# A decoder layer on one core: two buffers for the mixer's masked products, and level 0 of the next group issued before the finished group is weighed

## The reference, cut to what matters

```python
def step(S, inp):
    q_t, k_t, v_t, w_t = inp
    kv = k_t[..., :, None] * v_t[..., None, :]
    o_t = jnp.einsum('bhk,bhkv->bhv', q_t, S + u[None, :, :, None] * kv)
    S = jnp.exp(w_t)[..., None] * S + kv
    return (S, o_t)
```

## Time and profile before

| what | value |
|---|---|
| median of the runs | 1441.59 us (1439.81 to 1442.03) |
| the profiled execution's own time | 1454.23 us |
| span of that execution | 1452.4 us |
| PE busy | 1316.8 us, 91% of the span |
| DVE, POOL, ACT busy | 934.3, 746.1, 622.5 us |
| mean granted clock of PE | 0.967 |

### The profile page before, as it was taken

One profiled execution on the slowest core, in us unless ns is written; L12 is line 12 of the kernel. 1 busy time (PEld: TensorE's weight loads), 2 busy tenths in 40 slices (PEclk: granted clock), 3 DMA queues, 4 the chain that ended last, 5 costly groups with the idle time before them and its releaser, 6 DMA issues.

```text
span 1452.4 us, 30935 instructions
## 1 busy us (share of the span) xinstructions
PE 1316.8 (91%) x9852; PEld 889.5 (61%) x9853; DVE 934.3 (64%) x1964; ACT 622.5 (43%) x1519; POOL 746.1 (51%) x1080
## 2 busy tenths in 40 slices
PE   5789998999749999999999999999988999999996
PEld 3456655666535666666666666666655566666664
DVE  2587787777614888888888888888884322222221
ACT  2455544554313555555555555555543221211221
POOL 5234443243144678777787777877754322222222
PEclk9999999999757999999999999999999999999998
DMA  4996000000026554545544545545532322222221
GB/s 143 281 318 176 1 1 1 0 1 1 1 64 88 106 118 120 122 123 124 124 101 120 122 124 126 117 121 125 117 85 59 56 45 44 47 45 46 44 44 22
DMA packets 152749, 127.80 MB, mean 88 GB/s; under 512 B 41630, under 2 KB 145510, under 8 KB 152614
## 3 DMA queue, kind: packets, MB, share of 16 engines
q1 hardware_dynamic: 140310, 112.02, 31.3%
q0 software_dynamic: 12304, 14.10, 6.3%
HBM read 35.90 MB, written 44.83 MB: 56 GB/s over the span
## 4 chain that ended last, share of the span: by engine, by line
PE 56%; DVE 8%; issue 3%; ACT 2%; DMA 1%; SPq 0%; another core or an unknown queue 0%; POOL 0%; DVEq 0%; ACTq 0%; POOLq 0%
PE bank_st L1948 10%; PE bank_v L1966 7%; PE bank_s L1780 6%; PE bank_v L1768 6%; PE bank_o L1810 4%; PE bank_st L1790 4%; DVE neg_raw L1469 4%; PE bank_m L1743 4%; PE bank_s L1948 3%; PE bank_m L1832 2%; PE bank_st L1799 2%; DVE bank_st L1480 2%; PE bank_o L1957 2%; PE bank_v L1758 1%; PE bank_m L1820 1%
## 5 line engine op out<-in xcount | busy, mean ns | idle before, releaser
L1469 DVE TENSOR_REDUCE neg_raw<-bank_s 100x2 f32<-100x722 f32 x256 | 229.4, 896 | 32.1 <-PE bank_s L1780 30.2
L1316 ACT ACTIVATE prob<-bank_st 120x400 f32<-120x400 f32 (+1 forms) x384 | 166.2, 513 | 159.4 <-PE bank_st L1799 159.4
L1256 POOL DMA_INDIRECT out<-result,target x57 | 88.4, 1550 | 234.4 <-DVE result L1686 186.0
L1480 DVE TENSOR_SCALAR bank_st<-bank_st 121x1200 f32<-121x1200 f32 x128 | 180.3, 1408 | 1.2 <-PE bank_st L1790 0.8
L1681 DVE TENSOR_TENSOR hidden<-silu,bank_st 128x512 f32<-128x512 f32 x57 | 39.2, 688 | 192.7 <-PE bank_st L1948 192.7
L1948 PE MATMUL bank_st<-expert_w,rows_t 128*128 x344 | 159.3, 599 | 0.7 <-issue 0.5
L409 ACT ACTIVATE q_heads<-q 32x192 f32<-32x192 f32 (+3 forms) x224 | 82.7, 369 | 140.8 <-DVE q L521 136.4
L1780 PE MATMUL bank_s<-k_st,q_st 96*128 96x361 bf16 x512 | 124.1, 324 | 15.5 <-DVE neg_raw L1469 10.1
L1155 POOL TENSOR_TENSOR neg_diag<-xident_b,neg_max 100x400 bf16<-100x400 bf16 x128 | 109.4, 855 | 47.6 <-DVE neg_max L1474 47.0
L741 PE MATMUL bank_l<-q_heads,k 128*100 128x192 f32 (+4 forms) x512 | 114.9, 366 | 18.7 <-ACT q_heads L409 7.3
L293 POOL TENSOR_TENSOR mixed<-part,xn_t 128x400 f32<-128x400 f32 x80 | 84.4, 1080 | 82.0 <-DVE part L462 81.9
(11 more groups left out here) (231 smaller groups left out, 2545.8 us busy)
## 6 DMA issues: line engine op xcount, KB each, us to landing
k_st<-k_part SPq DMA_DIRECT2D x384, 90.2 KB
slot_rows<-empty SPq DMA_DIRECT2D x9, 2967.0 KB, 26.3
q_st<-q_part SPq DMA_DIRECT2D x192, 50.0 KB
kv<-in_ctx_t SPq DMA_DIRECT2D x32, 270.8 KB
expert_w<-in_w SPq DMA_DIRECT2D x16, 512.0 KB
rows<-slot_rows SPq DMA_DIRECT2D x57, 129.0 KB
residual<-in_w SPq DMA_DIRECT2D x16, 256.0 KB
residual<-in_x SPq DMA_DIRECT2D x8, 400.0 KB
```

Source lines behind the costliest of these rows:

```text
L1316: act.activation(prob[0:KEYS[c], t % 2, c], bank_st[0:KEYS[c], c, 0:4 * T], ACT.Exp).then_inc(exp_done, 1)
L1469: dve.tensor_reduce(neg_raw[:, h:h + 2], bank_s[0:T, :, 0:S], AX.X, ALU.max, negate=True).then_inc(max_done, 1)
L1480: dve.tensor_scalar(tile, tile, CLAMP, -CLAMP, ALU.min, ALU.max).then_inc(clipped, 1)
```

## The change

`attn` gets a second buffer, and a group uses the one of its parity `p`: in the diagonal copies, in the copies of the later levels and in `weigh`. The second buffer is cleared by GpSimd once, after its work for group 1's normalization, and VectorE waits for that before group 1. The diagonal copies of group g no longer wait for the weighing of g - 1 but for that of g - 2. On PE, `weigh` moves from the head of the body to behind level 0 of batches 0 and 1. On VectorE the diagonal copies of batches 0 and 1 move ahead of the statistics of the first bank. Nothing is added or taken away on PE or ScalarE. The diff, without the lines that only hand on `p`:

```diff
-        attn = sb("attn", [T, G, RH, T])
+        attn = sb("attn", [T, 2, G, RH, T])
...
-            pool.memset(attn[:], 0.0).then_inc(consts, 1)
+            pool.memset(attn[:, 0], 0.0).then_inc(consts, 1)
...
             norm(1)
+            pool.memset(attn[:, 1], 0.0).then_inc(consts, 1)
...
-            def collect(g, lv):
+            def collect(g, p, lv, batches=range(G)):
 
                 if lv == 0:
-                    for j in range(G):
+                    for j in batches:
                         dve.wait_ge(level_summed, g * LEVELS * G + j + 1)
-                        after(dve, o_summed, 2 * g)
+                        after(dve, o_summed, 2 * (g - 1))
                         dve.sem_inc(waited, 1)
-                        dve.copy_predicated(attn[:, j], diagonal[:].unsqueeze(1).to_broadcast([T, RH, T]),
+                        dve.copy_predicated(attn[:, p, j], diagonal[:].unsqueeze(1).to_broadcast([T, RH, T]),
...
+                    if isinstance(g, int) and g == 1 and s == 0:
+                        dve.wait_ge(consts, CONSTS + 1)
                     if s == 0 and not first:
+                        collect(g, p, 0, (0, 1))
                         head_stats(g - 1, 0)
-                    collect(g, s)
-                    if s == 0 and not first:
+                        collect(g, p, 0, (2, 3))
                         head_stats(g - 1, 1)
                         head_moments(g - 1)
+                    else:
+                        collect(g, p, s)
...
             def body(g, p, more):
                 first = isinstance(g, int) and g == 0
-                if not first:
-                    weigh(g - 1, 1 - p)
                 for s in range(LEVELS):
                     if s == 0 and not first:
                         level(g, p, 0, (0, 1))
+                        weigh(g - 1, 1 - p)
                         front(g, 7)
                         level(g, p, 0, (2, 3))
```

More of the change, by code:

```diff
@@ L549, in collect @@
                     src = bank_l[i][0:T, 0:8 * cols].rearrange("p (n c) -> p n c", n=8)
-                    dst = attn[:, 2 * i:2 * i + 2].rearrange("p b h t -> p (b h) t")
+                    dst = attn[:, p, 2 * i:2 * i + 2].rearrange("p b h t -> p (b h) t")
                     if lv == LEVELS - 1:
@@ L751, in weigh @@
                             mm = pe.matmul(bank_t[i][0:T, (j % 2) * D + h * RV:(j % 2) * D + (h + 1) * RV],
-                                           attn[:, j, h, :], val[:, p, j, h * RV:(h + 1) * RV], start=True, stop=True)
+                                           attn[:, p, j, h, :], val[:, p, j, h * RV:(h + 1) * RV], start=True, stop=True)
                     mm.then_inc(o_summed, 1)
```

## The result

The changed kernel is slower: 1451.87 us median (1450.09 to 1453.79, 4 runs) against 1441.07 us for the kernel before in the same comparison, a ratio of 1.0075 with a 95% interval of 1.006 to 1.009. That is 10.8 us; the forecast was 10.9 more, 1452.5 us.

What follows compares the result with a forecast made beforehand. PE, busy 91% of the span, was taken to bound the kernel. Seven boundary shifts (1.86 + 1.59 + 1.78 + 0.36 + 1.78 + 1.77 + 1.77 = 10.91 us) added to 1441.59 gave 1452.5 us, between 1448.6 and 1455.6.

Steps and rivals of the forecast that it cites:

- The covering work: At group boundaries, PE's weighing (2.87 us start to start before group 3) covers its wait for ScalarE's heads of level 0.
- The size of a shift: Per boundary, heads' end plus 0.20 us minus the weighing's old start: 1.59 to 1.86 us, except 0.36 at group 4.
- It stays: Every engine's next step at the boundary hangs on PE, so its 1.8 us shift passes to the whole rest of the group.
- At nothing: GpSimd's one-time clearing of the second buffer, during group 0, costs nothing; if VectorE waited, once and under 2 us.
- Group 4: At the loop's jump, copies ahead of the statistics remove a 1.07 us PE wait: shift 0.36 us instead of 1.59.
- A: Shift absorbed in PE's 3.56 us idle per group: no change, 1441 to 1443 us, or about 1447; chance 0.08.
- B: Heads ready in time, so only PE's copy waits (2.3 and 0.5 us) go: faster, 1438.8 us; chance 0.04.
- C: PE's clock falls at the boundaries, 1.9 us each: 1454.4 us at group 7 alone, 1465.7 at all seven; chance 0.08.

Runs made afterwards that it cites:

- e1: Changed kernel with PE's weighing put back ahead of level 0 of batches 0 and 1, buffers and VectorE order kept: 1440.60 us, ratio 0.9996 to the kernel before.
- e2: Kernel before, single buffer and old VectorE order, with only PE's move of level 0 of batches 0 and 1 ahead of the weighing: 1453.27 us, ratio 1.0076.
- e3: Changed kernel with the four level 0 head instructions on one batch of four, the other three batches left out: 1444.79 us, ratio 1.0024 to the kernel before.
- e6: Changed kernel with half of the weighing (8 matmuls) ahead of level 0 of batches 0 and 1, half behind: 1444.40 us, ratio 1.0011 to the kernel before.
- e4: Changed kernel with PE's move only in groups 1, 6 and 7, weighing first in groups 2 to 5: 1445.55 us, ratio 1.0027 to the kernel before.

## Why the prediction was right

*The covering work.* The prediction's main step, that the weighing is what PE does while the heads are made, held. Moving it away uncovered the wait in its full length; e1 and e2 put the whole cost on the move, e3 and e6 show that the wait follows the heads' end and the work ahead of it, one for one.

*The size of a shift.* 1.59 to 1.86 us were forecast and 1.64 to 1.75 found for the five plain boundaries up to group 6, and 1.64 for group 7 by itself, where 1.77 were forecast. The latency from the heads' end to PE was taken as 0.20 us from a place in group 5 and is 0.12 here (180.57 to 180.69). That the sum of 10.91 comes within 0.1 of the medians' 10.8 is in part luck: the interval is 8.6 to 13.0 us, and two pieces of the stage differ by 0.3 and 2.1 us between executions of one kernel.

*It stays.* The argument that every engine's next step at the boundary is released by PE held: the groups with the move lasted 46.4 to 46.65 us (forecast 46.6 to 46.8), those without, beside them in e4, 44.8 to 45.0 (45.6 with the loop's jump). "At nothing" for the clearing of the second buffer held too: among VectorE's waits from 36 to 90 us there is none for it.

*Group 4.* 0.36 was forecast, 0.34 found, but against the second profile of before (46.57) it would be 0.07, so the agreement of the number is luck. My reason was wrong as well: I ascribed the small shift to the copies being ahead of the statistics. In e2 they are not and the piece takes 46.69 us, as in the changed kernel (46.64). PE's own lateness hides the time of the jump.

*The rivals.* A fell to the group lengths, B to the wait of 1.56 us. C fell for groups 1 to 6: the gaps of 1.48 to 1.66 us left the granted clock at 1.00. At group 7 the rival stands. In the changed kernel's trace the gap of 2.17 us left the clock at 1.00 up to 370 us, and from 367 to 426 its mean is 0.74, as it is from 357 to 416 before. But in the traces of e2 and e4 a gap of 2.16 us at the same place was followed by a granted clock of 0.50, and level 1 came 1.66 and 1.58 us later, close to the 1.9 that C had for group 7. Group 7 with the rest of the stage lasts 66.2 to 66.9 us in the three traces with the move, 62.6 to 64.7 in three without (two of the kernel before, and e1). The difference is 1.5 to 4.3 us where the shift is 1.64. So the clock may add something to the cost in some executions, and how often is not known; the four runs of the changed kernel, 1450.09 to 1453.79, don't say.

*What was off.* I read the 12.64 us between the profiled execution and the median as a small factor on everything. It was one loss of about 10 us in the cross attention, in that execution only. It did little harm, because the sum came from the mixer's rows up to group 7, which agree between the two profiles of the kernel before but for the 0.27 us at the loop's jump.

## What to carry to other kernels

Before a piece of work is moved ahead of another on an in-order engine, compare the time at which its inputs are ready with the time at which it would start in its new place: a wait that costs nothing because other work stands ahead of it is paid in full when that work goes behind it. Making an instruction free to run earlier pays only if the bound engine waits for it or for what hangs on it; here that took a split of the projection, with which the copies of batches 2 and 3 started 1.3 us sooner. Before a second buffer is laid out for this, look whether the order of another engine doesn't already grant what it buys. And two profiles should be compared stage by stage: the totals of these two said the opposite of the timed runs.

## What was unexpected of the hardware

A ScalarE copy with a per-row scale takes 373 ns for 32x100 and 622 ns for 32x400, so a quarter of the columns takes 60% of the time; my estimate for e3 had drawn a line through forms without such a scale. The Trainium skill, "ScalarE: Activation LUTs", section "What ACT_TABLE_LOAD costs", gives 0.833 ns a column on top of a fixed part that grows with each per-row operand; by its figures an estimate is 362 and 612 ns, and the runs agree to within 11 ns.

The same gap of TensorE at the same place, 2.16 or 2.17 us before group 7, left the granted clock at 1.00 in one execution and was followed by 0.50 in two others, of kernels whose PE has the same instructions there. What decides it no run here shows.

And one execution of an unchanged stage took 10.4 us more than in the other profiles, in steps of 0.8 to 1.0 us about every second batch, with the granted clock and the instructions the same.
